# Causal attention: the row maxima run 34 score products ahead of the scores instead of 28

## The chip, the cores and the metric

The kernel runs on one core of one Trainium2 chip. The metric is device time in microseconds, the median of several runs. The engines are TensorE (PE, with its weight loads as PEld), VectorE (DVE), ScalarE (ACT), GpSimd (POOL) and SyncE (SP, which issues DMAs).

## What is computed

The program takes 16 images of 56 x 56 tokens with 32 channels through five residual layers: window attention, two token MLPs, and then twice a causal attention and an expert-choice layer. Each starts from a layer norm. The change concerns the two causal attentions, tags L2a and L3a, each over 3136 tokens per image with a single head of 32 channels:

```python
Q = embeddings @ W_Q
K = embeddings @ W_K
V = embeddings @ W_V
scores = jnp.einsum('bqd,bkd->bqk', Q, K) * (1.0 / jnp.sqrt(jnp.float32(d)))
masked = jnp.where(causal[None, :, :], scores, jnp.float32(-jnp.inf))
probs = jax.nn.softmax(masked, axis=-1)
out = jnp.einsum('bqk,bkd->bqd', probs, V)
t = t + out
```

## The kernel before

`causal_attention` cuts an image's tokens into seven blocks of queries, j = 0 to 6: six of 512 and a tail of 64. Keys come in tiles of 128. Every block needs its scores twice. First they are computed with queries on the partitions, so that VectorE can take the maximum over keys (kind "max", L425 on TensorE, L561 on VectorE). When the last maximum of a block is read, VectorE makes the negated maxima of the block (L583, L586 for the tail), and SP copies them with small DMAs into two rows of qT, eight DMAs for a block (L285 to L290). Then the scores are computed again with keys on the partitions (kind "score", L404); since qT now holds the negated maximum as one more channel, they come out shifted, and ScalarE takes the exponential at once (L529). Before the first score of a block TensorE waits for the block's shift, `shift_in`. GpSimd zeroes what lies above the diagonal (L363). The exponentials are multiplied with V in batches of up to 12 scores (kind "pv", L502), two accumulations of a block are joined ("acc": L540, L597), and "final" (L475, L479 for the tail, then L606, L608, L370) normalises and adds to the tokens.

The maxima of a block are: "edge", the four diagonal tiles in one bank, in which a product of a mask (kind "mask", L414) lies before; two "near" ones below the diagonal, shorter than 512 columns; and "far" ones of 512 x 128. The tail has six of 512 columns and its edge. An image has 84 scores and 85 maxima. Beside these, "vT" (transposes, L455) and "q" (L463) make the keys and queries of the next image, block by block, and ScalarE copies them (L546).

All score, maximum and helper products go through a ring of eight PSUM banks (RING), in the order in which they are written: a product waits until the product eight places before it has been read. The matrices have 32 rows, so four products can be in the array side by side: scores take the row groups 0 and 1, maxima 2 and 3.

The order on all engines is one list, WORK. Every item has a due time in units of scores, and the list is sorted by it. A score's time is its number. Maximum n has the time n * NS / NM - LEAD with NS = 1344 and NM = 1360. Items of two units are put together, so that two scores and two maxima usually stand together; such four are called a group here. A batch with V is due LAG = 6 scores after its last score. The edge maximum of a block is put to where a batch stands, so that mask and batch are neighbours. At the start of a stage, vT and q of the first image stand among maxima that run alone.

```python
LEAD, LAG, BATCH = 28, 6, 12

def max_time(n):
    return n * NS / NM - LEAD
```

An image has ten batches. In this text the stretch from the start of one batch to the start of the next has the name of its batch: P0, P1 and P2 for blocks 0 to 2 with one batch each, P3a and P3b, P4a and P4b, P5a and P5b for blocks 3 to 5 with two, and P6 for the tail.

Of the kernel before, what the change touches and what calls it, by code (L numbers as in the profile page):

```python
# [71 lines left out]
def causal_attention(nc, m, k, wq, wk, wv, eps, tag):  # L72
# [5 lines left out]
    TAIL = NJ - 1  # L78
    LT = NT - 1
    RING, RE = 8, 21  # L80
    LEAD, LAG, BATCH = 28, 6, 12

    def rows(t):
        return P if t < LT else LAST
# [1825 lines left out]
def program(nc, a, out):  # L1910

    with ExitStack() as ctx:
        k = make_constants(nc, ctx)
        m = Shared()
        m.NB = NB
        m.sem = lambda name: ctx.enter_context(nc.semaphore(name))
        m.T = ctx.enter_context(nc.sbuf_tensor("T", [P, NB + 1, NT, C], F32))
        m.mean = ctx.enter_context(nc.sbuf_tensor("mean", [P, NB + 1, NT], F32))
        m.rstd = ctx.enter_context(nc.sbuf_tensor("rstd", [P, NB + 1, NT], F32))
        clear_padding(nc, m)  # L1920
        window_attention(nc, m, k, a["L0_conv_w_qkv"], a["L0_conv_pos_emb"], a["L0_conv_w_out"],
                         a["L0_conv_b_out"], 1e-5, "win", load=lambda sp, i, loaded: load_image(m, a["x"], sp, i, loaded))
        token_mlps(nc, m, k, {n[8:]: t for n, t in a.items() if n.startswith("L1_conv_")}, 1e-5, "mlp")
        for layer, wq, wk, wv in (("L2", "W_Q", "W_K", "W_V"), ("L3", "Wq", "Wk", "Wv")):
            causal_attention(nc, m, k, *(a[f"{layer}_attn_{w}"] for w in (wq, wk, wv)), 1e-5, f"{layer}a")
            expert_choice(nc, m, k, *(a[f"{layer}_ffn_{w}"] for w in ("gate_w", "gate_b", "weight1", "weight2")),
                          f"{layer}f")
        store_images(nc, m, out)
# [31 lines left out]
```

How the kernel before makes its waits and increments, by code:

```python
        @block.gpsimd  # L45
        def _(pool):
            nc.gpsimd.memset(k.ident[:], 0.0).then_inc(made, 1)
            nc.gpsimd.memset(k.mask_qk[:], 0.0).then_inc(made, 1)
            nc.gpsimd.memset(k.mask_kq[:], 0.0).then_inc(made, 1)
            nc.gpsimd.memset(k.basis[:], 0.0).then_inc(made, 1)
            pool.wait_ge(made, 4)
            nc.gpsimd.affine_select(out=k.ident[:], in_=k.ident[:], compare_op=ALU.not_equal, fill=1.0,
                                    base=0, pattern=[[-1, P]], channel_multiplier=1).then_inc(made, 1)
            nc.gpsimd.affine_select(out=k.mask_qk[:], in_=k.mask_qk[:], compare_op=ALU.is_ge, fill=NEG,
# [2 lines left out]
                                    base=-3 * P, pattern=[[1, 4 * P]], channel_multiplier=-1).then_inc(made, 1)  # L57
            nc.gpsimd.affine_select(out=k.basis[:].rearrange("p (r c) -> p r c", r=4),
                                    in_=k.basis[:].rearrange("p (r c) -> p r c", r=4),
                                    compare_op=ALU.not_equal, fill=1.0,
                                    base=0, pattern=[[0, 4], [-1, C]], channel_multiplier=1).then_inc(made, 1)
            pool.wait_ge(made, 8)
            nc.gpsimd.memset(k.basis[0:1, :], -1.0).then_inc(made, 1)
            nc.gpsimd.tensor_copy(k.ident_bf[:], k.ident[:]).then_inc(made, 1)
            pool.wait_ge(made, 10)
            nc.gpsimd.memset(k.basis[:, 0:4 * C:C], 0.0).then_inc(made, 1)
            pool.wait_ge(made, 11)
```

## Time and profile before

| | us |
|---|---|
| median of 3 runs | 4711.13 (4706.0 to 4712.59) |
| the profiled execution | 4710.27 |
| its span | 4708.6 |
| first attention, from first to last batch | 1373.46 |
| second attention, from first to last batch | 1368.46 |

Over the whole span PE is busy for 4141.0 us (88%), DVE for 3134.4 (67%), ACT for 2752.3 (58%) and POOL for 1430.2 (30%). The two attentions are 58% of the span. The shares are averages over layers with different limits, so the stretches of a stage are read apart. A view of the timeline merges instructions of a kind that follow each other; one product of 32-bit floats is recorded as two matmuls (x2), and some matmul records are missing. The end of a matmul is modelled: where a start is followed by a long idle time, the distance of starts says more than the ends.

### The profile page before, as it was taken

What the parts mean: (1) busy time and instruction counts of PE and PEld (TensorE: products, weight loads), DVE (VectorE), ACT (ScalarE), POOL (GpSimd) and SP (SyncE); (2) the same over time, 40 slices, a digit from 0 to 9 for tenths busy, and PEclk for the clock granted to TensorE, in tenths of its full rate; (3) what the DMA queues carried; (4) which work ended last, traced back from release to release, by engine and by line L of the source; (5) the groups of instructions that cost most, each with busy time, mean ns of one, the idle gap of its engine ahead of it and who ended that gap; (6) DMA issues with size and microseconds to landing.
All of it is one profiled execution on the core that took longest, in us unless ns stands there. A gap on an engine that the chain in (4) does not pass through costs nothing. (4 is left out here: it accounts for less than half of the span.)

```text
span 4708.6 us, 125775 instructions
## 1 busy us (share of the span) xinstructions
PE 4141.0 (88%) x51290; PEld 2867.8 (61%) x51290; DVE 3134.4 (67%) x6164; ACT 2752.3 (58%) x5706; POOL 1430.2 (30%) x2222
## 2 busy tenths in 40 slices
PE   3888888888686799999999999779999999999975
PEld 2666666666332466666676666456666666666754
DVE  4777777777798466666666666536666666666653
ACT  2777777776586355655655555415555556556541
POOL 4333223321000343433433432122433434334220
PEclk9999999999798699999999999769999999999987
DMA  1200000000000000000000000000000000000003
GB/s 25 33 3 3 2 2 3 2 2 2 3 1 1 1 2 2 2 2 3 2 3 2 2 2 2 6 1 2 2 2 2 3 2 2 2 2 2 3 6 55
DMA packets 348272, 24.07 MB, mean 5 GB/s; under 512 B 346388, under 2 KB 347700, under 8 KB 347700
## 3 DMA queue, kind: packets, MB, share of 16 engines
q1 hardware_dynamic: 347700, 16.03, 4.7%
q8 instruction: 409, 6.70, 0.6%
q14 instruction: 163, 1.34, 0.1%
HBM read 7.88 MB, written 6.42 MB: 3 GB/s over the span
## 5 line engine op out<-in xcount | busy, mean ns | idle before, releaser
L561 DVE TENSOR_REDUCE L2a_mx<-L2a_r 128x1 f32<-128x512 f32 (+4 forms) x1344 | 760.8, 627 | 243.4 <-PE L2a_r L425 240.3
L561 DVE TENSOR_REDUCE L3a_mx<-L3a_r 128x1 f32<-128x512 f32 (+4 forms) x1344 | 760.5, 627 | 239.8 <-PE L3a_r L425 236.4
L529 ACT ACTIVATE L2a_e<-L2a_r 128x512 f32<-128x512 f32 (+3 forms) x1344 | 658.8, 579 | 284.9 <-PE L2a_r L404 282.7
L529 ACT ACTIVATE L3a_e<-L3a_r 128x512 f32<-128x512 f32 (+3 forms) x1344 | 658.6, 579 | 280.5 <-PE L3a_r L404 278.5
L425 PE MATMUL L2a_r<-L2a_vT,L2a_qT 32*128 32x512 f32 (+3 forms) x3488 | 817.6, 529 | 0.0
L425 PE MATMUL L3a_r<-L3a_vT,L3a_qT 32*128 32x512 f32 (+3 forms) x3488 | 815.0, 528 | 0.1
L404 PE MATMUL L2a_r<-L2a_qT,L2a_vT 32*128 32x512 f32 (+4 forms) x3488 | 779.8, 518 | 29.4 <-DMA L2a_qT<-L2a_nm 29.4
L404 PE MATMUL L3a_r<-L3a_qT,L3a_vT 32*128 32x512 f32 (+4 forms) x3488 | 777.6, 516 | 27.3 <-DMA L3a_qT<-L3a_nm 27.3
L1454 POOL TENSOR_SCALAR win_xw<-win_xr,win_mv,win_rs 32x343 f32<-32x343 f32 (+7 forms) x432 | 327.9, 779 | 703.3 <-ACT win_rs L1242 703.2
L404 PEld LDWEIGHTS L2a_r<-L2a_qT,L2a_vT 32*128 32x128 f32 x3488 | 372.1, 188 | 189.3 <-issue 100.3
L404 PEld LDWEIGHTS L3a_r<-L3a_qT,L3a_vT 32*128 32x128 f32 x3488 | 370.6, 187 | 186.8 <-issue 98.9
L425 PEld LDWEIGHTS L2a_r<-L2a_vT,L2a_qT 32*128 32x128 f32 x3488 | 394.0, 194 | 51.0 <-DVE L2a_mx L561 24.3
L425 PEld LDWEIGHTS L3a_r<-L3a_vT,L3a_qT 32*128 32x128 f32 x3488 | 390.8, 192 | 51.0 <-DVE L3a_mx L561 25.0
L502 PEld LDWEIGHTS L2a_r<-L2a_e,L2a_v 128*32 128x32 f32 x10400 | 302.5, 111 | 118.9 <-ACT L2a_e L529 100.3
L502 PEld LDWEIGHTS L3a_r<-L3a_e,L3a_v 128*32 128x32 f32 x10400 | 302.3, 111 | 119.1 <-ACT L3a_e L529 100.3
L502 PE MATMUL L2a_r<-L2a_e,L2a_v 128*32 128x128 f32 x10400 | 347.1, 273 | 3.9 <-POOL L2a_e L363 3.1
L502 PE MATMUL L3a_r<-L3a_e,L3a_v 128*32 128x128 f32 x10400 | 346.5, 273 | 4.1 <-POOL L3a_e L363 3.3
L1106 PE MATMUL win_mx<-win_mk,win_xw 113*64 113x196 f32 x2048 | 202.7, 339 | 134.1 <-issue 126.5
L1268 ACT COPY win_yb<-win_yp 64x512 f32<-64x512 f32 x256 | 148.3, 579 | 237.5 <-PE win_yp L1190 236.0
L1220 ACT COPY win_mq<-win_pq 32x392 f32<-32x392 f32 x512 | 246.6, 482 | 57.3 <-PE win_pk L1099 50.1
L363 POOL TENSOR_SCALAR_AFFINE_SELECT L2a_e<-L2a_e 128x128 f32<-128x128 f32 (+2 forms) x304 | 98.8, 326 | 581.2 <-ACT L2a_e L529 567.5
L363 POOL TENSOR_SCALAR_AFFINE_SELECT L3a_e<-L3a_e 128x128 f32<-128x128 f32 (+2 forms) x304 | 98.8, 326 | 576.8 <-ACT L3a_e L529 563.0
(370 smaller groups left out, 6745.0 us busy)
## 6 DMA issues: line engine op xcount, KB each, us to landing
L2a_qT<-L2a_nm SPq DMA_DIRECT2D x768, 0.5 KB, 2.0
L3a_qT<-L3a_nm SPq DMA_DIRECT2D x768, 0.5 KB, 2.0
T<-in_x SPq DMA_DIRECT2D x16, 384.0 KB, 3.7
out<-T SPq DMA_DIRECT2D x16, 384.0 KB, 4.0
win_mq<-win_nmt SPq DMA_DIRECT2D x256, 3.1 KB, 1.7
win_msk<-in_L_conv_pos_emb SPq DMA_DIRECT2D x49, 0.2 KB
L2a_qT<-L2a_nm SPq DMA_DIRECT2D x32, 0.2 KB, 1.8
L3a_qT<-L3a_nm SPq DMA_DIRECT2D x32, 0.2 KB, 1.8
```

Of the source, the lines that this page charges most:

```text
L363: nc.gpsimd.affine_select(out=e, in_=e, compare_op=ALU.is_ge, fill=0.0, base=0, pattern=pattern, channel_multiplier=-1).then_inc(mask_done, 1)
L404: last = nc.tensor.matmul(bank_of(x)[0:r, o:o + c1 - c0], VT[g0:g0 + C, img % 2, u * P:u * P + r], QT_[g0:g0 + C, img % 2, j * QB + c0:j * ...
L425: return nc.tensor.matmul(bank_of(x)[:, o:o + c1 - c0], QT_[g0:g0 + C, img % 2, q0:q0 + P], VT[g0:g0 + C, img % 2, c0:c1], start=start, st ...
L502: last = nc.tensor.matmul(bank[C * i:C * i + C, 0:b - a], V[0:r, img % 2, u, :], E[0:r, n % RE, o + a:o + b], start=u == same[0], stop=u = ...
L529: nc.scalar.activation(E[0:r, n % RE, 0:w], bank_of(x)[0:r, 0:w], ACT.Exp).then_inc(exp_done, 1)
L561: return nc.vector.tensor_reduce(to, frm, AX.X, ALU.max)
L1106: last = nc.tensor.matmul(bank[half * SLOT:(half + 1) * SLOT, c0:c0 + HK], window(n, 2 * p + half), buf[:, slot, half, p].rearrange("p h c ...
L1220: last = nc.scalar.copy(MQ[0:C, q_slot(n), :, :, h, :], PQ[h * C:(h + 1) * C, 0:NW * K].rearrange("p (w f c) -> p f w c", f=2, c=K))
L1268: last = nc.scalar.copy(YB[r, n % 2, :, :, half, :].rearrange("p a h c -> p (a h) c"), YP[r, :].rearrange("p (a c) -> p a c", c=C))
L1454: last = nc.gpsimd.tensor_scalar(dst, s, MV[:, 0:1], RS[:], ALU.subtract, ALU.mult)
```

## The change

One number of the planner changes: the due time of every maximum is six scores, that is three groups, earlier.

```diff
     RING, RE = 8, 21
-    LEAD, LAG, BATCH = 28, 6, 12
+    LEAD, LAG, BATCH = 34, 6, 12
```

No instruction's kind or size changes. What moves is shown at two places.

The first is VectorE in the middle of an image of the first attention, from the final of block 2 (`RECIPROCAL`, `TENSOR_TENSOR L2a_ot`) to the negated maxima of the tail (L586). `TENSOR_TENSOR L2a_o` is the add of block 3's second batch in P3b, `L2a_mx` and `L2a_mt` are maxima of blocks and of the tail, and the `L2a_nm` of L583 are the negated maxima of block 5. Before:

```order
L606 RECIPROCAL L2a_rd<-L2a_r 128x4
L608 TENSOR_TENSOR L2a_ot<-L2a_r,L2a_rd 128x128
L561 TENSOR_REDUCE L2a_mx<-L2a_r 128x1 x8
L597 TENSOR_TENSOR L2a_o<-L2a_o,L2a_r 128x128
L561 TENSOR_REDUCE L2a_mx<-L2a_r 128x1 x7
L583 TENSOR_REDUCE L2a_nm<-L2a_mx 128x4
L561 TENSOR_REDUCE L2a_mt<-L2a_r 64x1 x3
L606 RECIPROCAL L2a_rd<-L2a_r 128x4
L608 TENSOR_TENSOR L2a_ot<-L2a_r,L2a_rd 128x128
L561 TENSOR_REDUCE L2a_mt<-L2a_r 64x1 x4
L586 TENSOR_REDUCE L2a_nm<-L2a_mt 64x1
```

After:

```order
L606 RECIPROCAL L2a_rd<-L2a_r 128x4
L608 TENSOR_TENSOR L2a_ot<-L2a_r,L2a_rd 128x128
L561 TENSOR_REDUCE L2a_mx<-L2a_r 128x1 x8
L597 TENSOR_TENSOR L2a_o<-L2a_o,L2a_r 128x128
L561 TENSOR_REDUCE L2a_mx<-L2a_r 128x1
L583 TENSOR_REDUCE L2a_nm<-L2a_mx 128x4
L561 TENSOR_REDUCE L2a_mt<-L2a_r 64x1 x7
L586 TENSOR_REDUCE L2a_nm<-L2a_mt 64x1
```

Between the add and the negated maxima of block 5 stand one maximum instead of seven, and the tail's maxima all stand before the next final.

The second is TensorE in P6, from its transposes of the next image's keys (L455) to the q product (L463) and the batch of block 0 behind it (L502). Before:

```order
L455 MATMUL L2a_r<-ident,L2a_vr 128x128 x4
L414 MATMUL L2a_r<-mask_qk,ident_bf 128x512
L404 MATMUL L2a_r<-L2a_qT,L2a_vT 128x512 x2
L425 MATMUL L2a_r<-L2a_vT,L2a_qT 128x512
L425 MATMUL L2a_r<-L2a_vT,L2a_qT 128x128 x4
L404 MATMUL L2a_r<-L2a_qT,L2a_vT 128x384
L404 MATMUL L2a_r<-L2a_qT,L2a_vT 128x256
L404 MATMUL L2a_r<-L2a_qT,L2a_vT 128x128
L425 MATMUL L2a_r<-L2a_vT,L2a_qT 128x128
L425 MATMUL L2a_r<-L2a_vT,L2a_qT 128x384
L425 MATMUL L2a_r<-L2a_vT,L2a_qT 128x256
L463 MATMUL L2a_r<-L2a_vT,L2a_A 128x512
```

After:

```order
L455 MATMUL L2a_r<-ident,L2a_vr 128x128 x4
L404 MATMUL L2a_r<-L2a_qT,L2a_vT 128x512 x2
L425 MATMUL L2a_r<-L2a_vT,L2a_qT 128x512 x2
L404 MATMUL L2a_r<-L2a_qT,L2a_vT 128x384
L404 MATMUL L2a_r<-L2a_qT,L2a_vT 128x256
L404 MATMUL L2a_r<-L2a_qT,L2a_vT 128x128
L425 MATMUL L2a_r<-L2a_vT,L2a_qT 128x512 x2
L463 MATMUL L2a_r<-L2a_vT,L2a_A 128x512
L502 MATMUL L2a_r<-L2a_e,L2a_v 32x128 x10
```

The mask, block 4's edge maximum (four of 128 columns) and the near maxima of block 5 have left P6 for the stretch before it, and four whole maxima stand in their place.

## Rows read from the trace of the kernel before

**Rows 1.** By stretch: length; busy PE, PEld, DVE, ACT, POOL (instructions); PEclk, DMA, GB/s.
```profile
1609.15:2982.61 1373.46, 1331.83 (x18154) 938.76 (x18154) 883.27 (x1788) 795.05 (x1713) 480.68 (x815) 0.98 0.05 2
...
3177.36:4545.82 1368.46, 1328.84 (x18154) 935.59 (x18154) 883.23 (x1788) 794.68 (x1713) 480.73 (x815) 0.98 0.05 2
```
**Rows 2.** A wait over the whole span: us in total, times, longest us.
```profile
PE L2a_r L404 <- DMA L2a_qT<-L2a_nm: 29.4, 16, 2.3
```
**Rows 3.** Timeline of TensorE in one P4a: start, length, instructions [idle before <-releaser].
```profile
2172.57 2.39 PE L502 MATMUL L2a_r<-L2a_e,L2a_v 128*32 128x128 f32 x68
...
2175.78 0.70 PE L404 MATMUL L2a_r<-L2a_qT,L2a_vT 32*128 32x512 f32 x2
...
2176.32 0.59 PE L404 MATMUL L2a_r<-L2a_qT,L2a_vT 32*128 32x512 f32 x2
...
2176.75 1.02 PE L404 MATMUL L2a_r<-L2a_qT,L2a_vT 32*128 32x512 f32 x2
2178.88 0.66 PE L404 MATMUL L2a_r<-L2a_qT,L2a_vT 32*128 32x512 f32 x1 [1.12 <-DMA L2a_qT<-L2a_nm]
```
**Rows 4.** Timeline of VectorE, negated maxima of block 5 in two images.
```profile
2172.10 0.18 DVE L583 TENSOR_REDUCE L2a_nm<-L2a_mx 128x4 f32<-128x28 f32 x1
...
2687.15 0.18 DVE L583 TENSOR_REDUCE L2a_nm<-L2a_mx 128x4 f32<-128x28 f32 x1
```
**Rows 5.** Timeline of TensorE, block 5's first score in the second of them.
```profile
2695.13 0.66 PE L404 MATMUL L2a_r<-L2a_qT,L2a_vT 32*128 32x512 f32 x1 [2.32 <-DMA L2a_qT<-L2a_nm]
```
**Rows 6.** By stretch, P4a: two of 32, and each attention's sum of 16.
```profile
2000.02:2014.35 14.33, 12.40 (x133) 7.85 (x132) 7.13 (x18) 7.44 (x17) 5.75 (x11) 0.88 0.06 3
...
2172.57:2184.50 11.93, 10.81 (x133) 7.11 (x132) 7.14 (x18) 7.40 (x17) 5.76 (x11) 1.00 0.07 2
...
sum 212.72, PE 183.36 PEld 119.15 DVE 111.62 ACT 116.13 POOL 82.04; mean PE 11.46 PEld 7.45 DVE 6.98 ACT 7.26 POOL 5.13
...
sum 208.60, PE 181.32 PEld 116.70 DVE 111.54 ACT 115.63 POOL 82.20; mean PE 11.33 PEld 7.29 DVE 6.97 ACT 7.23 POOL 5.14
```
**Rows 7.** Timelines around one P6: VectorE's maxima, TensorE's q; the stretch itself.
```profile
1957.52 1.68 DVE L561 TENSOR_REDUCE L2a_mx<-L2a_r 128x4 f32<-128x512 f32 x4
...
1958.27 1.12 PE L463 MATMUL L2a_r<-L2a_vT,L2a_A 32*128 32x512 f32 x2 [0.82 <-DVE L2a_mx L561]
...
1953.24:1959.32 6.08, 5.26 (x86) 3.49 (x86) 4.31 (x11) 3.24 (x8) 1.44 (x4) 1.00 0.02 1
...
L463 PE MATMUL L2a_r<-L2a_vT,L2a_A 32*128 32x512 f32 x180 | 95.8, 626 | 11.5 <-DVE L2a_mx L561 11.5
```
**Rows 8.** Busy time by stretch, P0: some of 32, and each attention's sum.
```profile
1609.15:1617.48 8.33, 8.33 (x57) 5.95 (x58) 2.58 (x4) 3.50 (x7) 0.60 (x2) 0.64 0.04 0
...
1959.32:1965.68 6.36, 6.36 (x47) 3.35 (x46) 2.73 (x6) 3.32 (x8) 0.24 (x1) 0.73 0.10 3
2047.81:2052.70 4.89, 4.89 (x48) 2.65 (x47) 2.74 (x6) 3.33 (x8) 0.24 (x1) 1.00 0.12 3
...
sum 89.54, PE 89.54 PEld 49.40 DVE 43.89 ACT 51.88 POOL 4.71; mean PE 5.60 PEld 3.09 DVE 2.74 ACT 3.24 POOL 0.29
...
3177.36:3185.18 7.82, 7.82 (x57) 5.27 (x57) 2.48 (x4) 3.48 (x7) 0.61 (x2) 0.72 0.04 0
...
sum 88.34, PE 88.34 PEld 48.46 DVE 43.56 ACT 51.42 POOL 4.73; mean PE 5.52 PEld 3.03 DVE 2.72 ACT 3.21 POOL 0.30
```
**Rows 9.** Timeline of TensorE, maxima at the first attention's start.
```profile
1598.41 1.06 PE L425 MATMUL L2a_r<-L2a_vT,L2a_qT 32*128 32x512 f32 x2
...
1599.26 1.06 PE L425 MATMUL L2a_r<-L2a_vT,L2a_qT 32*128 32x512 f32 x2
```
**Rows 10.** Whole maxima of VectorE, grouped by line (mean ns); one P5a by stretch.
```profile
L561 DVE TENSOR_REDUCE L2a_mx<-L2a_r 128x1 f32<-128x512 f32 x935 | 584.0, 684 | 115.2 <-PE L2a_r L425 114.9
...
1934.91:1946.47 11.56, 11.56 (x183) 9.54 (x181) 8.46 (x17) 5.87 (x14) 0.68 (x2) 1.00 0.08 3
```
**Rows 11.** The page's costliest groups: the batches with V of one attention.
```profile
L502 PE MATMUL L2a_r<-L2a_e,L2a_v 128*32 128x128 f32 x10400 | 347.1, 273 | 3.9 <-POOL L2a_e L363 3.1
```

## The prediction

> **What bounds the kernel now.** I read the profile in this order: the stretches of the two attention stages, the waits of TensorE, then the program order of one image laid beside the timeline.
>
> The two stages take 1373.46 and 1368.46 us, and TensorE is busy for 97% of both, at a mean granted clock of 0.98 [rows 1]. VectorE is busy for 64% and ScalarE for 58%. So TensorE sets the time, and a microsecond in which it stands still is lost, unless VectorE or ScalarE is also late there. The reader should look for the little time in which TensorE is not busy, and for the 2% of clock.
>
> The waits name one large cause: scores wait for the shift (the DMA that copies the negated maxima into qT), 16 times and 29.4 us in the first stage [rows 2], and much the same in the second. That is once per image. The program order says where: in stretch P4a, at the first score of block 5. A block's lead is 28 scores less the number of its own maxima, since the maxima of block 5 (22 products and the edge) are themselves spread over as many scores. So block 5, the largest, has the shortest lead, some 5 scores.
>
> One such place in time: the batch of products with V begins at 2172.57, score products follow 0.43 us apart (2176.32 to 2176.75), the next would have come at 2177.18, but TensorE goes on at 2178.88 [rows 3]. VectorE had finished the negated maxima of block 5 at 2172.10 + 0.18 = 2172.28 [rows 4]. From there to the score are 6.60 us: eight small DMAs, issued one after the other. This is the shortest of the 32 chains; the longest runs from 2687.33 to 2695.13, 7.80 us [rows 4, 5].
>
> The stall has a second cost. Where the stall is long, the granted clock falls to its lower level, 1.2 GHz, for a while behind it: the stretch 2000.02 to 2014.35 has a mean of 0.88 and 12.40 us of TensorE busy, against 10.81 in 2172.57 to 2184.50 with the same instructions at 1.00 [rows 6].
>
> A second, smaller wait stands in P6. The product that makes q of the next image's block 0 (L463) waits 0.82 us for VectorE, 14 times in a stage [rows 7]. Its PSUM bank is, eight places back in the ring, the one that the edge maximum of block 4 occupies from the mask on, and VectorE reaches that only after four more steps. The stretch takes 6.08 us every time, and after it, in P0, the clock is sometimes at its lower level: 6.36 us at 0.73 against 4.89 at 1.00 [rows 8].
>
> **The change part by part.** No instruction is added or removed; every maximum stands three groups (a group is two scores and two maxima) earlier among the scores. What else moves follows from that, as the order shows.
>
> *The wait for the shift.* On VectorE the negated maxima of block 5 now stand 6 reductions nearer to the add before them. At 684 ns by the row of a reduction [rows 10] that is 4.1 us, so the lead grows from 2177.18 - 2172.28 = 4.90 us to about 9.0, where the chains want 6.60 to 7.80. TensorE has slightly more to do in front of that score too (two masks move into P3b). I take the wait as gone in all 32 images, with 1.2 us to spare in the worst. The tail's maxima and the next image's first blocks follow closely on SP's queue, behind block 5's chain and not in front of it, and their scores come much later.
>
> What P4a then costs: 11.93 us less the standstill 2178.88 - 2177.18 = 1.70 gives 10.2; taking off only the recorded idle of 1.12 gives 10.8 [rows 3, 6]. I take 10.2, since the distance of 0.43 is read in this very stretch. The 32 stretches take 212.72 + 208.60 = 421.3 us [rows 6]. Gain: 421.3 - 32 x 10.2 = 95 us, or 421.3 - 32 x 10.8 = 76 by the other bound. This holds the clock's share, since stretches without a stall run at 1.00.
>
> *The wait in P6.* Block 4's edge maximum goes one stretch earlier with its mask, and P6 has four whole maxima instead. Eight places in front of the q product now stands a score, which ScalarE empties early. The wait of 0.82 us goes, and TensorE also saves the drain before it, as the 0.6 us between the two figures of P4a. Bounds: nothing (if the edge maximum makes the last group of P5b wait instead, where it now stands behind a whole one, one reduction later), and 0.82 + 0.6 = 1.4 us. I take 1.0, nearer to the recorded wait: 30 stretches, 30 us, with 0 and 42 as ends.
>
> *The clock in P0.* The sums are 89.54 and 88.34; without the first image of each stage (8.33 and 7.82) 161.7 us for 30 stretches, and 30 x 4.89 would be 146.7 [rows 8]. If P6 has no standstill, 15 us go; if it keeps one, none.
>
> *Maxima against other batches.* P3b gets two masks and the edge maxima; P4a loses a mask; P4b, P5a and P1 get whole maxima in place of the short near ones. Maxima and masks per image stay the same in sum, so this is nothing on TensorE. Where a stretch goes by VectorE, a whole maximum in place of a short one shows: I estimate 0.1 us in each of P5a and P1, 2 x 0.1 x 32 = 6 us more. The bounds are one reduction less or more per image, 32 x 0.684 = 22 us each way. GpSimd's work keeps its place beside the scores, except for the second image's first statistics, which come some maxima later in the start, where it waits anyway.
>
> *The start and the end.* Six more maxima stand in front of the first score of a stage. There TensorE runs at the lower clock, and such maxima come 0.85 us apart (1598.41 to 1599.26) [rows 9]: 6 x 0.85 x 2 = 10 us more. At the end of each stage six scores stand without maxima beside them, which gives back some; I take 2 us, since ScalarE has the same exponentials there. Net +8, with +4 and +10 as bounds.
>
> Sum: -95 - 30 - 15 + 6 + 8 = -126 us. The profiled execution took 4710.27 us (its span 4708.6), 0.9 below the median of the three runs, 4711.13, so I set the sum against the median: 4711 - 126 = 4585 us.
>
> **The rivals.**
>
> *Only the shift's wait goes.* In P6 the wait moves to P5b or to P0, and the clock there stays as it is. For it: the ring has eight banks, and the edge maximum holds its bank from the mask on wherever it stands. Against it: VectorE idles about a third of the stage. 4711 - 95 + 6 + 8 = 4630 us.
>
> *The clock stays low at times.* The falls in P0 and P4a would not be due to the two waits but to the ring's smaller ones. In P4a the falls cost 14 x 1.6 = 22 us (14 of its 32 stretches lie below 1.00, each taken as 12.40 against 10.81 [rows 6]), in P0 15. Against it: P5a, with most maxima in a row, runs at 1.00 with its bank waits [rows 10]. Time: 4585 + 22 + 15 = 4622 us. The Trainium skill (TensorE: Matmul & The Clock Gate, A second HAM failure mode: psum-queue depth-cycling) tells of a kernel that cycles through PSUM banks and whose clock swings because TensorE idles briefly between groups. By that rule the falls would stay; the trace disagrees so far, since this kernel cycles through eight banks too and P5a shows 1.00.
>
> *Slower: VectorE becomes the pace.* An image has 42 groups, each of which gives VectorE up to two reductions, 2 x 0.684 = 1.37 us [rows 10]. Now it catches up beside the batches and in the very stalls that go. If it no longer did, because the eight banks are full when a batch begins, an image would take 42 x 1.37 = 57.5 us for groups, 347.1 / 16 = 21.7 for batches [rows 11], seven times 0.82 for what stands behind a batch (2174.96 to 2175.78 [rows 3]) and seven times 0.43 for q: 87.9 us. Now it takes (1373 + 1368) / 32 = 85.7. That would be 4711 + 32 x 2.2 + 8 = 4789 us. It decides from (85.7 - 30.4) / 42 = 1.32 us per group. Against it: even in P5a VectorE is busy for 8.46 of 11.56 us only [rows 10].
>
> *Part of the stall stays.* If the chain grew past 9 us, because SP is still busy with the block before, 32 times some 1 to 2 us and part of the clock would remain: 4585 + 32 to 64, and up to 22 more, 4617 to 4671 us. Against it: block 4's negated maxima stand more than 15 reductions earlier, over 10 us, where the longest chain takes 7.80.
>
> **How the numbers follow.** The forecast, 4545 to 4611 about 4585, gets 0.55. Only the shift's wait goes, 4612 to 4650: 0.20. The clock stays low at times, about 4622: 0.07. More than forecast, below 4545, which needs the -22 of the moved maxima or all the better bounds: 0.05. Part of the stall stays: 0.06. No gain at all, since something else is late at the same places: 0.03. VectorE as the pace: 0.04. The range from 4545 to 4650 takes in the bounds of the terms (95 or 76, 42 or 0) and leaves out 0.18. A measurement of this kernel can tell about 0.2%, 9 us, from no change. Faster by more than that: 0.93, the first five cases. Within it 0.03, slower 0.04.
>
> **What would show it.** In the profile after, no wait of L404 for the DMA into qT in either stage; P4a at 9 to 10.8 us with a clock of 1.00; P6 at 4.5 to 5.3 us without the 0.82; P0 at 4.9 everywhere; the first score some 5 us later after the first maximum. It is wrong if TensorE waits for the shift at another block, if P3b or P5a grow by more than 1 us, or if the granted clock of the stages stays at 0.98.

## The result and the profile after

The changed kernel takes 4595.9 us (4594.31 to 4597.48, four runs) where the kernel before takes 4710.6 us beside it: a ratio of 0.9758, interval 0.9741 to 0.9775. The forecast was 4585 us, with a range of 4545 to 4650. The span of the profiled execution goes from 4708.6 to 4593.2 us.

First the stretches of the changed kernel: the two stages, the start of the first stage (from VectorE's first maximum to the first batch), and then one P0, P3b, P4a, P5b, P6 and P1 of one image (times and columns as in [rows 1]; line numbers stay).

```profile
1615.39:2923.89 1308.50, 1289.17 (x18142) 922.01 (x18142) 877.93 (x1782) 795.46 (x1713) 480.77 (x815) 1.00 0.05 2
3122.05:4430.61 1308.56, 1289.03 (x18142) 921.65 (x18142) 877.99 (x1782) 795.39 (x1713) 480.74 (x815) 1.00 0.05 2
1568.20:1615.39 47.19, 45.05 (x169) 23.31 (x167) 28.72 (x54) 10.34 (x22) 10.18 (x12) 0.57 0.05 1
1700.51:1705.39 4.88, 4.88 (x47) 2.65 (x46) 3.61 (x8) 3.44 (x9) 0.78 (x3) 1.00 0.01 3
1731.44:1741.18 9.74, 9.30 (x125) 6.12 (x125) 6.56 (x14) 6.33 (x14) 5.69 (x11) 1.00 0.06 3
1741.18:1751.18 10.00, 10.00 (x130) 7.65 (x129) 6.95 (x19) 6.84 (x17) 4.30 (x8) 1.00 0.09 3
1771.35:1778.42 7.07, 6.25 (x133) 4.55 (x131) 4.13 (x9) 1.85 (x4) 0.99 (x3) 1.00 0.02 2
1778.42:1783.17 4.75, 4.75 (x80) 2.93 (x76) 3.37 (x7) 3.55 (x8) 0.91 (x3) 1.00 0.11 1
1788.05:1799.18 11.13, 11.13 (x121) 7.76 (x121) 7.82 (x17) 8.38 (x19) 3.21 (x7) 1.00 0.04 2
```

The stages shrink from 1373.46 and 1368.46 us [rows 1] to 1308.5 each, and the granted clock, 0.98 before, is 1.00. P4a takes 10.00 us and is not idle; before it took 11.93 to 15.23. P6 takes 4.75 instead of 6.08 [rows 7] (in the image before a stage's last, 3.49 instead of 4.59), and P0 takes 4.88 in every image but the first of a stage, where before it was 6.36 at times [rows 8]. Three stretches got longer: P1, which took 10.83 before, P3b and P5b. The rows of before of the last two are these:

```profile
1904.32:1912.90 8.58, 8.58 (x114) 5.98 (x113) 6.38 (x13) 5.95 (x15) 4.63 (x10) 1.00 0.01 3
...
1946.47:1953.24 6.77, 6.77 (x132) 5.08 (x130) 3.97 (x7) 2.34 (x5) 0.99 (x3) 1.00 0.06 3
```

P3b grew by 1.16 us and P5b by 0.30, and these two now have a little time in which TensorE is not busy: 0.44 and 0.82 us. The waits of TensorE over the whole span say for whom in P5b (us in total, times, longest; the row that answers to [rows 2], the wait for the DMA into qT, is gone in both attentions):

```profile
PE L2a_r L404 <- DVE L2a_mx L561: 12.3, 15, 0.8
PE L3a_r L404 <- DVE L3a_mx L561: 12.3, 15, 0.8
```

The timelines around both places, VectorE and TensorE in P3b, then in P5b (its row at 1776.61 is block 4's edge maximum), and between them the first score of block 5 in P4a:

```profile
1735.16 0.69 DVE L561 TENSOR_REDUCE L2a_mx<-L2a_r 128x1 f32<-128x512 f32 x1 [1.30 <-PE L2a_r L425]
1735.88 0.18 DVE L583 TENSOR_REDUCE L2a_nm<-L2a_mx 128x4 f32<-128x28 f32 x1
1736.10 1.44 DVE L561 TENSOR_REDUCE L2a_mt<-L2a_r 64x1 f32<-64x64 f32 x3
...
1736.38 0.69 PE L463 MATMUL L2a_r<-L2a_vT,L2a_A 32*128 32x512 f32 x1 [0.44 <-DVE L2a_mt L561]
...
1745.97 0.59 PE L404 MATMUL L2a_r<-L2a_qT,L2a_vT 32*128 32x512 f32 x2
...
1775.67 0.69 DVE L561 TENSOR_REDUCE L2a_mx<-L2a_r 128x1 f32<-128x512 f32 x1 [1.04 <-PE L2a_r L425]
1776.40 0.17 DVE L583 TENSOR_REDUCE L2a_nm<-L2a_mx 128x4 f32<-128x20 f32 x1
1776.61 0.69 DVE L561 TENSOR_REDUCE L2a_mx<-L2a_r 128x4 f32<-128x512 f32 x1
...
1777.35 0.70 PE L404 MATMUL L2a_r<-L2a_qT,L2a_vT 32*128 32x512 f32 x2 [0.82 <-DVE L2a_mx L561]
```

The reader should see two things. The negated maxima of block 5 are ready at 1735.88 + 0.18 = 1736.06. The first score of block 5, the fourth after the batch as in [rows 3], starts at 1745.97, 9.91 us after them (its exponential 11.11), and waits for nothing; before it started 6.60 us after them at the least, and had waited. In the last image of a stage the lead is shorter: there the exponential comes 9.01 us after the negated maxima. And both new waits have one shape: an edge maximum, whose bank is taken from the mask on, now stands behind a whole maximum and the negated maxima on VectorE, and the product that is to have the bank next waits. In P3b it is the tail's edge, in P5b block 4's.

Added up over all images of both stages, before to after, the change in us is: P4a and P4b of the last images and P4a of the others -96.0 - 15.6, P6 -39.5, P0 -15.9, P4b -13.5, P3b +34.6, P5b +9.2, P1 +10.1, the starts +11.4 (41.63 and 41.37 to 47.19 twice), P5a and P5b of the last images +1.6. The sum is -113.5; the span is 115.4 shorter, and the rest of that lies outside these stretches. The spells of the lower clock in the stages, counted in the trace, go from 26 (12 in P0, 14 in P4a) to none, apart from one in a stage's first P0 and one in each stage's last P5a.

### The profile page after: what moved, and what is told of

Read it like the earlier page. It is cut to its first block and busy times, and to the rows that moved or that the text cites. A ratio compares the mean times of both kernels' runs of the same rounds, so it can differ in the third digit from the quotient of the medians.

```text
span 4593.2 us, 125713 instructions
## 1 busy us (share of the span) xinstructions
PE 4068.9 (89%) x51290; PEld 2839.0 (62%) x51290; DVE 3131.4 (68%) x6164; ACT 2753.2 (60%) x5706; POOL 1430.3 (31%) x2222
## 5 line engine op out<-in xcount | busy, mean ns | idle before, releaser
L404 PE MATMUL L3a_r<-L3a_qT,L3a_vT 32*128 32x512 f32 (+4 forms) x3488 | 756.7, 505 | 12.7 <-DVE L3a_mx L561 12.3
L404 PE MATMUL L2a_r<-L2a_qT,L2a_vT 32*128 32x512 f32 (+4 forms) x3488 | 756.4, 505 | 12.7 <-DVE L2a_mx L561 12.3
L425 PEld LDWEIGHTS L3a_r<-L3a_vT,L3a_qT 32*128 32x128 f32 x3488 | 377.5, 189 | 43.4 <-issue 18.6
L425 PEld LDWEIGHTS L2a_r<-L2a_vT,L2a_qT 32*128 32x128 f32 x3488 | 376.8, 188 | 43.3 <-issue 18.3
L502 PEld LDWEIGHTS L2a_r<-L2a_e,L2a_v 128*32 128x32 f32 x10400 | 300.9, 110 | 107.9 <-ACT L2a_e L529 84.2
L502 PEld LDWEIGHTS L3a_r<-L3a_e,L3a_v 128*32 128x32 f32 x10400 | 300.0, 110 | 108.1 <-ACT L3a_e L529 84.2
L502 PE MATMUL L2a_r<-L2a_e,L2a_v 128*32 128x128 f32 x10400 | 344.0, 272 | 2.1 <-POOL L2a_e L363 2.1
L502 PE MATMUL L3a_r<-L3a_e,L3a_v 128*32 128x128 f32 x10400 | 343.0, 271 | 2.4 <-POOL L3a_e L363 2.4
L363 POOL TENSOR_SCALAR_AFFINE_SELECT L3a_e<-L3a_e 128x128 f32<-128x128 f32 (+2 forms) x304 | 98.8, 325 | 547.0 <-ACT L3a_e L529 533.1
L1106 PEld LDWEIGHTS win_mx<-win_mk,win_xw 113*64 113x64 f32 x2048 | 158.1, 138 | 179.6 <-issue 178.3
```

The lines of the kernel that those rows point to most:

```text
L363: nc.gpsimd.affine_select(out=e, in_=e, compare_op=ALU.is_ge, fill=0.0, base=0, pattern=pattern, channel_multiplier=-1).then_inc(mask_done, 1)
L404: last = nc.tensor.matmul(bank_of(x)[0:r, o:o + c1 - c0], VT[g0:g0 + C, img % 2, u * P:u * P + r], QT_[g0:g0 + C, img % 2, j * QB + c0:j * ...
L425: return nc.tensor.matmul(bank_of(x)[:, o:o + c1 - c0], QT_[g0:g0 + C, img % 2, q0:q0 + P], VT[g0:g0 + C, img % 2, c0:c1], start=start, st ...
L502: last = nc.tensor.matmul(bank[C * i:C * i + C, 0:b - a], V[0:r, img % 2, u, :], E[0:r, n % RE, o + a:o + b], start=u == same[0], stop=u = ...
L1106: last = nc.tensor.matmul(bank[half * SLOT:(half + 1) * SLOT, c0:c0 + HK], window(n, 2 * p + half), buf[:, slot, half, p].rearrange("p h c ...
```

## Experiments

The theory is that of the prediction: two waits of TensorE cost the time, block 5's shift in P4a and the bank of block 4's edge maximum in P6, and each also costs some clock; the six scores of lead take both away. The rivals are that the gain comes from the distance of all maxima, in proportion, or that the clock gains whatever goes. Times stand beside the kernel before on the same chip: 4708.8 for the three other leads and for block 4's edge alone, 4713.3 for the kernels with fewer or more DMAs and for the edge back in P6, and 4718.5 for the last four.

**The distance itself.** The constant alone, at 30, 32 and 36.

```diff
-    LEAD, LAG, BATCH = 34, 6, 12
+    LEAD, LAG, BATCH = 30, 6, 12      # and 32, and 36
```

> The planner's lead is 30 instead of 28. Theory (the gain is mostly the wait for block 5's shift, which ends when the lead exceeds the chain of 6.6 to 7.8 us): the lead of block 5 grows from 4.9 us by two reductions, 1.4, to 6.3, so a rest of 0.3 to 1.5 us of the wait stays in each image, P4a is at 10.5 to 12 us with some falls of the clock, and P6 loses most of its 0.82, since the edge maximum stands first in its group: 4640 to 4670 us. Rival (the gain comes from where masks and batches fall at 34, not from the shift): no steady change, 4700 to 4720.

> Lead 32. Theory of the shift: the lead of block 5 is 4.9 + 4 x 0.69 = 7.6 us against chains of 6.6 to 7.8, so the wait is gone in nearly all images: 4590 to 4615 us, P4a near 10 us at a clock of 1.00. Rival (the gain is in proportion to the lead): two thirds of the 115 us, 4634.

> Lead 36. Theory of the shift: nothing is left to gain from it, so only the arrangement counts; in P5b the edge maximum of block 4 stands first in its group again, so the 0.82 us that P5b has at 34 goes (30 x 0.3 to 0.8 us), and two more maxima stand in front (2 x 2 x 0.85 = 3 us): 4575 to 4595 us. Rival (in proportion to the lead): a further 38 us less, 4558. Rival (deeper is worse, VectorE becomes late): above 4600.

Measured: 4619.8 us (0.9812, 0.9787 to 0.9837), 4603.4 (0.9777, 0.9752 to 0.9802) and 4600.5 (0.9771, 0.9746 to 0.9796). Against 28 to 30, which brings 89 us, 30 to 32 brings 16, 32 to 34 some 8 or less, and 34 to 36 nothing: a threshold and not a slope. With 30 the chain just about fits: block 5's first exponential comes 7.7 to 8.9 us after the negated maxima, where it came 7.7 to 9.6 us after them before, but the waits list a single wait for the DMA in both attentions, of 0.21 us, where the kernel before had 32 of up to 2.3, and the spells of the lower clock are as in the changed kernel. So 30 came out below the 4640 to 4670 that were expected. A P4a of it:

```profile
1905.76:1916.38 10.62, 10.62 (x133) 7.39 (x133) 6.83 (x18) 6.87 (x16) 5.09 (x10) 1.00 0.08 2
```

So two scores of lead do nearly all for the shift, and the other four are worth what else falls out of the order. From 28 to 30, P4a gives 81 us and P6 26. The 16 from 30 to 32 are not the shift: P4a stays at 10.8 and 10.7, and P4b, where with 30 TensorE waits 0.50 us for a bank, goes from 9.67 to 8.77. P6 is 5.20 with 30 and 32, and 4.75 with 34 and 36. A further gain with 36 (4575 to 4595) was expected and did not come, and 4600.5 lies where the rival of a late VectorE put it, though TensorE waits for no bank of a maximum there. Its start takes 48.98 us, and of the stretches only P3b (9.53) and P5b (6.50) are shorter than with 34, while P4a (10.33), P4b (9.04) and P1 (11.24) are longer. Why they are was not separated.

**Block 4's edge alone.** The maxima at 28 again; only block 4's edge maximum and its mask go to the next batch, that of P0.

```diff
-            spot, at = spots[0] if spots else (len(MAXES), max_time(len(MAXES)) - 2)
+            spot, at = spots[1 if j == 4 and len(spots) > 1 else 0] if spots else (len(MAXES), max_time(len(MAXES)) - 2)
```

> Lead 28 as before, but the edge maximum of block 4 and its mask go with the batch P0 instead of P6. Theory (P6 stands for that edge maximum's bank, and the falls of the clock in P0 follow from that standstill): P6 takes 4.7 us instead of 6.1, P0 takes a mask more (5.2 to 5.7) without falls of the clock, P4a stays as before at 12 to 14.7 us: 4711 - 40 + 15 - 15 = 4655 to 4685 us. Rival (the falls in P0 have another cause): P0 still has means of 0.73 in some ten images, 15 us more than that.

Measured: 4684.8 us, 0.9944 (0.9925 to 0.9963). One P4a, P6 and P0 each, and the wait:

```profile
1910.94:1924.36 13.42, 11.92 (x134) 8.20 (x133) 7.24 (x18) 7.24 (x17) 5.40 (x10) 0.87 0.06 2
1951.74:1956.49 4.75, 4.75 (x80) 3.15 (x79) 3.30 (x10) 3.09 (x8) 0.91 (x3) 1.00 0.00 2
1956.49:1961.74 5.25, 5.25 (x54) 3.41 (x53) 3.73 (x9) 3.49 (x8) 0.78 (x3) 1.00 0.12 4
...
PE L2a_r L404 <- DMA L2a_qT<-L2a_nm: 26.1, 16, 2.1
```

P6 lost its wait and 1.33 us, and the clock no longer falls in P0. P6 gave 39.5 us in all. P0 gave 4.1 in the images after the first, although it now holds the mask and the edge maximum and takes 5.25 instead of 4.88. But P4a grew by 19.4, since its stall is still there and the lower clock came with it in 28 of 32 images, where before it did so in 14. So the falls of P0 do follow the standstill of P6, and yet a fall that is taken away there can turn up behind the next one.

**Block 5's shift alone.** The maxima at 28; block 5's shift is made with four DMAs instead of eight, and the second row of qT is left out for that block, so its scores lack a part of the shift.

```diff
-        return 32 * (img * NT + min(QT * (j + 1), NT))
+        return 32 * (img * NT + min(QT * (j + 1), NT)) - 64 * (img + (j >= 5))
...
-                            for g0 in (0, C):
+                            for g0 in ((0, C) if j != 5 else (0,)):
```

> Lead 28 as before, but block 5's shift is copied by four DMAs instead of eight, into one of the two rows of qT (the copy into the other row is left out for block 5, so half of its scores are not shifted). Theory (the 32 stalls are block 5's chain of DMAs on SP): the chain shortens by some 2.6 us, below the lead of 4.9, the stall goes without any maximum moved: P4a 10.0 to 10.8 us at a clock of 1.00, about 90 us less, 4610 to 4630 us. P6 keeps its 0.82 and its 6.08 us; if the falls of the clock in P0 come from that wait, some ten means of 0.73 stay there (15 us); if they needed the stall in P4a as well, P0 is 4.88 throughout and the time is at 4600 to 4615. Rival (the stall is not the chain but where the scores stand): 4700 or more.

Measured: 4608.3 us, 0.9785 (0.9762 to 0.9808). One P4a, one P6 and one P0:

```profile
1903.00:1913.45 10.45, 10.45 (x133) 7.18 (x132) 7.14 (x18) 7.33 (x17) 5.76 (x11) 1.00 0.04 2
1940.82:1946.91 6.09, 5.27 (x87) 3.49 (x86) 4.31 (x11) 3.25 (x8) 1.45 (x4) 1.00 0.02 1
2280.32:2286.79 6.47, 6.47 (x48) 3.33 (x47) 2.74 (x6) 3.33 (x8) 0.24 (x1) 0.74 0.08 1
```

No maximum moved, and most of the gain is there: the span is 97.2 us shorter and the stages 96.5, of which 92.3 are in P4a, 5.2 in the last P4b and 2.1 in P0, less some 3 in P5a and P5b of the last images (by the medians it is 105 us). Where the clock is high, the score comes 4.90 us after the negated maxima, just the lead that the prediction read from the order, and the wait is gone, while P6 keeps its 0.82 and P0 its falls (13 spells, none in P4a). This is the price of the shift's wait by itself.

**The chain lengthened in the changed kernel.** Ahead of block 5's eight DMAs stand two or eight more, into a scratch row that nobody reads. Beside the lines shown, the scratch row is added and `shifts` counts the DMAs added.

```diff
+                        for i in range(8 if j == 5 else 0):      # or 2
+                            sp.dma_start(SCR[0:1, i], NM_[P - r:P, img % 2, j, 0:1],
+                                         allow_slow_non_contiguous=True).then_inc(shift_in, 16)
```

> Lead 34 as in the kernel after, with two more DMAs of 128 values to an unused place in front of block 5's eight: its chain grows by some 1.3 us, to 7.9 to 9.1. Theory (lead of 34: first score of block 5 about 9.9 us behind the negated maxima): no wait appears, 4590 to 4602 us, P4a 10.0. Rival (the lead of 34 only just covers the chain): a wait in some images, 4605 to 4640.

> Lead 34 with eight such DMAs in front: the chain grows by some 5.2 us to 11.8 to 13, which is 2 to 3 us past the lead of about 9.9. Theory: the wait of the scores for the shift is back in P4a in all 32 images, P4a 12 to 14.5 us with falls of the clock, 32 x (2 to 3.5): 4660 to 4710 us. Rival (the shift's chain does not matter once the order has changed): 4596.

Measured: with two 4600.7 us, 0.9769 (0.9746 to 0.9792), P4a at 10.00 and no wait in any image but the last of each stage, where the lead is shorter: there the score waits 0.62 and 0.33 us, and starts 9.0 and 8.7 us after the negated maxima. With eight 4708.0 us, 0.9991 (0.9979 to 1.0003). With eight, the waits (lines are four higher here), and one P4a, P6 and P0:

```profile
PE L2a_r L408 <- DMA L2a_qT<-L2a_nm: 35.9, 16, 3.8
...
1913.57:1927.70 14.13, 12.19 (x130) 8.99 (x129) 7.04 (x18) 6.84 (x16) 4.07 (x8) 0.76 0.10 3
1954.95:1959.70 4.75, 4.75 (x80) 2.93 (x77) 3.37 (x7) 3.55 (x8) 0.91 (x3) 1.00 0.12 4
1959.70:1964.58 4.88, 4.88 (x47) 2.65 (x46) 3.60 (x8) 3.44 (x9) 0.78 (x3) 1.00 0.01 2
```

With eight the score starts 11.9 to 13.1 us after the negated maxima, more than the lead of 9.91, and the whole gain is gone, although every maximum stands where the change put it and P6 and P0 are as short as in the changed kernel. Apart from the first P0 and the last P5a, the lower clock comes in 25 spells, all in P4a. The wait is longer than it was in the kernel before, 35.9 against 29.4 us in the first attention, so this shows that the chain alone can undo the gain, and not that the two amounts are the same.

**The new waits.** In P5b and P3b an edge maximum holds a bank. First block 4's edge is sent back to P6, in the changed kernel (the edit of the edge, above); then the tail's edge, and then both, go one place later in VectorE's list:

```diff
             spot, at = spots[0] if spots else (len(MAXES), max_time(len(MAXES)) - 2)
+            if j in (6,):      # or (4, 6)
+                spot += 1
+                at = max_time(spot) - 2
```

> Lead 34, but the edge maximum of block 4 and its mask are put back to the batch of P6, first in its group, instead of behind a whole maximum in P5b. Theory (a product waits for the edge maximum whose bank is eight places back): the 0.82 us in P5b goes, P5b takes 6.4 instead of 7.07, P6 5.2 instead of 4.75 (the mask's 0.3 and a short wait): 32 x 0.2 less, 4585 to 4595 us, and no fall of the clock. Rival (P6 with a mask is as before, 6.08 with falls of the clock behind it): 4620 to 4640.

> Lead 34, but the edge maximum of the tail goes one place later, first in the second group of P3b, with its mask in front of that group. Theory (P3b grew by 1.16 us, of which 0.44 is q's wait for the bank that the tail's mask holds until VectorE has read a whole maximum and then the edge): the wait goes and P3b takes 9.2 to 9.4 us instead of 9.74, 30 x 0.4 = 12 us less than the kernel after. Rival (VectorE is late there anyway, q's wait is only where it shows): P3b 9.7, the same time.

> As the run before, and block 4's edge maximum also one place later, first in the second group of P5b. Theory (its 0.82 us is a wait for its bank too): P5b takes 6.4 to 6.7 instead of 7.07, P6 stays at 4.75, in sum 12 + 30 x 0.5 = 27 us less than the kernel after, 4569 us: faster than both kernels. Rival: the mask between the groups costs what the wait cost, 4584 to 4596.

> The kernel after once more, so that the next three have it on the same chip: 4594 to 4601 us, each stretch as in its first profile.

Measured: the edge back in P6 4600.9 us, 0.9769 (0.9747 to 0.9791); the other two 4588.1, 0.9724 (0.969 to 0.9758), and 4580.3, 0.9709 (0.9675 to 0.9743), where the changed kernel takes 4595.4 beside them. First P5b and P6 with the edge back in P6, then P3b and P5b with both edges later:

```profile
1936.90:1943.69 6.79, 6.79 (x126) 4.74 (x124) 4.30 (x10) 2.88 (x6) 0.99 (x3) 1.00 0.03 3
1943.69:1948.89 5.20, 5.20 (x84) 3.59 (x83) 3.29 (x7) 2.66 (x7) 1.05 (x4) 1.00 0.12 5
```
```profile
1897.50:1906.96 9.46, 9.46 (x125) 6.37 (x124) 6.64 (x15) 6.31 (x14) 5.44 (x11) 1.00 0.07 5
1937.13:1943.93 6.80, 6.80 (x133) 4.69 (x132) 4.30 (x10) 2.66 (x6) 1.00 (x3) 1.00 0.02 3
```

The edge back in P6 takes the wait in P5b away and gives it back as work: 6.79 + 5.20 = 11.99 us, against 7.07 + 4.75 = 11.82, so the 4585 to 4595 expected of it were missed. One place later, both waits go and no stretch takes them over: P3b 9.46 instead of 9.74, P5b 6.80 instead of 7.07, P6 still 4.75. The expected 4569 was missed: of a wait of 0.44 the stretch gives back 0.28, and of one of 0.82 only 0.27. TensorE's busy time grows as the wait goes, in P3b from 9.30 to 9.46 and in P5b from 6.25 to 6.80: it does the same work in less time when it goes on after the wait. The last version is faster than both kernels.

**Both causes without the change.** The maxima at 28, with block 4's edge in P0 and block 5's shift by four DMAs, the second row again left out.

> Lead 28 with both causes taken away and no other maximum moved: four DMAs instead of eight for block 5 (half of its shift is left out), and block 4's edge maximum in P0. Theory (the change's gain is the shift's wait, the wait in P6 and their falls of the clock, less what the new arrangement and the longer start cost): P4a 10.45, P6 4.75, P0 5.25, all at a clock of 1.00, 82.2 us per image and no longer start: 4711 - 32 x 2.7 - 30 x 1.33 + 30 x 0.37 - 15 = 4560 to 4585 us, that is faster than the kernel after by 15 to 35. Rival (the earlier maxima gain something of their own): 4600 or more.

Measured: 4570.8 us, 0.9689 (0.9655 to 0.9723). P4a, P6 and P0 of one image:

```profile
1900.27:1910.72 10.45, 10.45 (x134) 7.20 (x133) 7.14 (x18) 7.34 (x17) 5.79 (x11) 1.00 0.05 2
1938.09:1942.85 4.76, 4.76 (x80) 3.16 (x79) 3.32 (x10) 3.11 (x8) 0.92 (x3) 1.00 0.01 2
1942.85:1948.10 5.25, 5.25 (x55) 3.41 (x54) 3.74 (x9) 3.49 (x8) 0.78 (x3) 1.00 0.12 4
```

With neither wait no spell of the lower clock is left in P0 or P4a. The two causes together are worth more than the change: it takes 25 us more. So the earlier maxima bring nothing by themselves; beyond what they unblock they cost. The stretches say where: the starts +11.4, P3b +34.6, P1 +10.1, P5b +9.2, against P4a -13.8, P4b -13.5 and P0 -12.4.

## Why the prediction was right

*The wait for the shift, taken at 95 us (76 to 95).* Right in mechanism, and the size came out with some luck. The wait is gone in all 32 images. Taken alone it is worth 97 us, and made long again it costs all of the gain. But without the stall P4a takes 10.45 us and not 10.2, 8 us less gain in thirty images, and the last images, which the sum took like the others, give 10 us more in P4a and P4b than the sum had from them. The lead was forecast at about 9.0 us and is 9.91. On VectorE the negated maxima end 2.21 us after the add in place of 5.88, a gain of 3.67 where the sum had 4.1; the other 1.3 are TensorE's, which now reaches the score that much later after the add. The prediction had named that ("slightly more to do in front of that score") without a number. In the last image of a stage the score comes some 7.8 us after the negated maxima (the 9.01 of its exponential less the 1.20 between the two elsewhere), which only just covers the chain, so the 1.2 us to spare in the worst case were not there. Nor did the falls of the clock in P4a go by the length of the stall, as the prediction had it: in the kernel before, a wait of 1.12 us was followed by one, and a wait of 2.32 us was not. P4a came out at 10.00, against 10.2 in the sum. The 0.45 us between 10.45 (28, no stall) and 10.00 is moved work, as the row of P4a has three matmuls fewer than [rows 6] and that of P3b eleven more than before.

*P6, taken at 30 (0 to 42).* Measured 39.5, near the upper bound: 28 stretches are 1.33 us shorter, and two, which took 4.59 us before and not 6.08, are 1.10 shorter. Not all of it is the wait: with mask and edge maximum back in P6 and no wait (the edge back in P6, above) it takes 5.20. So 0.88 of the 1.33 are the wait, 26 us in all and a little less than the 1.0 that was taken, and 0.45, 14 us in all, is work that left P6. The lower bound's mechanism happened all the same: block 4's edge makes the last group of P5b wait 0.82 us behind a whole maximum. It costs P5b only 0.30, 9.2 us in all.

*The clock in P0, 15.* Measured 15.3 in the same 30 stretches. The link to P6's standstill is borne out by two kernels: the falls are gone with P6's wait at a lead of 28, and they stay with it when only P4a's stall goes.

*Maxima against other batches, +6 (22 either way).* This is the term that was mis-sized. P3b +34.6, P1 +10.1, P5b +9.2, less P4b 13.5 and less the 14 of P4a's moved work, are +26, above the upper bound; with the 14 of P6's moved work taken off as well it is +12, inside the bounds and twice the +6. The working said that masks and maxima stay the same in sum, "so this is nothing on TensorE"; but P3b now holds 14 of VectorE's instructions instead of 13 and 125 matmuls instead of 114, and it pays for them more than P4a and P4b save. Of its 1.16 us, 0.28 are the wait for the tail's edge, and of P5b's 0.30 nearly all is the wait for block 4's. Where the rest of P3b's growth comes from was not separated. The prediction had named a growth of P3b above 1 us as a sign that it is wrong. The sign came, and for this term it was right; it did not touch the others.

*The start, +10, and the end, -2.* The starts took 11.4 us more (5.56 and 5.82 each). The end gave nothing of its own: the last images' P4a and P4b are 15.6 us shorter, but so they are, by 15.1, with the shift's wait alone gone, and their P5a and P5b took 1.6 more.

So -97 - 39.5 - 14 (P0 without the 2 that the shift takes there) + 26 + 11 is about -114 us, against a forecast of -126. With all moved work in one term it is -97 - 26 - 14 + 12 + 11: the shift's wait brought 2 us more than forecast, P6's wait 4 less and the clock 1 less, and the moved maxima cost 6 more and the starts 3 more.

*The rivals.* That only the shift's wait goes (4630) falls with P6 at 4.75. VectorE as the pace falls with 877.93 us of 1308.50 and 82.7 us for an image. That part of the stall stays happened in no image, and the kernel with eight DMAs more shows its price: all of it comes back. That the clock stays low at times is refuted: the granted clock is 1.00 although TensorE waits 0.44 and 0.82 us for a bank in 15 of the 16 images of each stage. P5a, which the prediction set against this rival, was no test of it: TensorE is busy there for all of the 11.56 us [rows 10]. The Trainium skill (TensorE: Matmul & The Clock Gate, A second HAM failure mode: psum-queue depth-cycling) tells of a clock that swings with small gaps at the change of PSUM banks; by that rule the falls would have stayed, and here the trace disagrees.

## What to carry to other kernels

Read, for each product that waits for a chain on other engines, how long the chain takes and how much lead the order gives it: the gain of a longer lead ends where the lead passes the chain, here between 28 and 30, and what lies beyond only moves work about. Before all work is moved earlier, look whether the one item that is late can be moved, or its chain made shorter. In a ring of banks, ask of each moved item what it stands behind on the engine that empties its bank: one place in that order decided whether a bank was waited for.

## What the runs showed of the hardware

The same length of standstill had different consequences. In P6, 0.82 us for a bank was followed in 12 of 28 images by the lower clock (P0 at 0.73 [rows 8], 0.74 above); in P5b of the changed kernel 0.82 us for a bank, in 15 images of each stage, was followed by 1.00 throughout. What tells the two apart was not found; the recorded idle time was the same, but P6 lost 0.88 us by it (6.08 against 5.20) and P5b 0.27 (7.07 against 6.80). In P4a the falls did not go by the length of the wait (1.12 us with one, 2.32 us without). Nor are they a fixed price of a place: with P6's wait gone and P4a's stall kept, their number stayed (28 against 26), and all stood in P4a.

A chain of small DMAs on one queue took 6.6 to 7.8 us for eight, from the end of its producer to the start of its consumer, and 11.9 to 13.1 us for sixteen: some 0.66 us for each one more. With ten it took 8.7 and 9.0 us in the two images that waited for it. With four the consumer, at 4.90 us, did not wait.
